# Eight score units of a second cross attention moved ahead of a linear layer, its first maxima placed between FFN tiles, and its third pack loaded under other waits

## The reference, cut to what matters

```python
x = x + L0_xattn(layernorm(x), ctx)          # self attention, cross attention, FFN (relu), norms g1, g2, g3
x = x + L0_ffn(layernorm(x))                 # a linear layer with a low rank part: "lin"
x = x + L1_xattn(layernorm(x), ctx, ctx, pad_mask, subsq_mask)   # the second cross attention
x = x + L1_ffn(layernorm(x))                 # experts: gated q, k, v products, attention, gated MLP
# L1_xattn: 16 heads of 16, scores / 4, masked places -1e9, softmax over T = 77 keys, times v
```

## Time and profile before

| | |
|---|---|
| runs before | median 1295.17 us (1292.96 to 1298.21, 3 runs) |
| profiled execution | 1296.56 us, span 1294.8 us, granted PE clock 0.942 |
| busy in the span | PE 1130.4 us (87%), DVE 834.1 (64%), ACT 556.0 (43%), POOL 261.0 (20%) |
| chain that ended last | PE on L726 12% of the span, DVE 0% |

### The profile page before, as it was taken

The page is one execution under the profiler, slowest core; times in us unless marked ns, Lnnn a source line. Parts: engine busy times, 40 slices in busy tenths (PEclk is TensorE's granted clock), DMA queues, the critical chain, the costliest instruction groups (busy, mean ns, idle before and its releaser), DMA issues. The chain is left out here.

```text
span 1294.8 us, 19733 instructions
## 1 busy us (share of the span) xinstructions
PE 1130.4 (87%) x6996; PEld 768.3 (59%) x6996; DVE 834.1 (64%) x1820; ACT 556.0 (43%) x1199; POOL 261.0 (20%) x429
## 2 busy tenths in 40 slices
PE   8789899988978788989868588899989788899999
PEld 4444333333333336667644256799978677789988
DVE  5486777877754667856654586676544566865555
ACT  6215666655646545445425343320023333543342
POOL 5012222222221045533212500000010113300000
PEclk8889999999989869999988789999989999999999
DMA  6750373330544502005615400001030000000000
GB/s 211 176 135 2 58 65 51 51 51 2 99 53 73 114 10 70 1 1 88 70 14 164 77 10 1 1 1 33 1 130 2 1 1 1 1 17 1 17 17 17
DMA packets 51217, 61.05 MB, mean 47 GB/s; under 512 B 16794, under 2 KB 40880, under 8 KB 50608
## 3 DMA queue, kind: packets, MB, share of 16 engines
q1 hardware_dynamic: 50688, 56.64, 22.6%
q0 software_dynamic: 432, 3.15, 0.7%
HBM read 44.02 MB, written 15.15 MB: 46 GB/s over the span
## 5 line engine op out<-in xcount | busy, mean ns | idle before, releaser
L726 PE MATMUL PS<-ARENA 128*17 128x512 f32 (+14 forms) x1720 | 299.4, 449 | 46.5 <-DVE ARENA L2062 15.5
L1585 ACT ACTIVATE ARENA<-PS 128x512 f32<-128x512 f32 (+3 forms) x384 | 169.9, 495 | 134.5 <-PE PS L726 132.3
L2062 DVE TENSOR_REDUCE ARENA<-PS 128x1 f32<-128x128 f32 (+7 forms) x256 | 182.7, 751 | 45.5 <-PE PS L726 43.7
L726 PEld LDWEIGHTS PS<-ARENA 128*17 128x17 f32 (+5 forms) x1720 | 87.6, 101 | 195.3 <-issue 107.1
L726 PE MATMUL PS<-WQKVP,TRR 128*128 128x384 f32 x512 | 137.8, 351 | 8.7 <-DVE ARENA L2323 7.4
L2515 POOL TENSOR_SCALAR_AFFINE_SELECT ARENA<-ARENA 128x128 f32<-128x128 f32 x256 | 74.0, 299 | 224.8 <-ACT ARENA L1585 222.9
L726 PEld LDWEIGHTS PS<-WQKVP,TRR 128*128 128x128 f32 x512 | 91.8, 191 | 17.9 <-DVE ARENA L2323 9.5
L726 PEld LDWEIGHTS PS<-W2P,INT 128*128 128x128 f32 x768 | 95.3, 188 | 2.9
L2483 POOL TENSOR_TENSOR rstd<-var,halves 128x4 f32<-128x4 f32 x36 | 38.4, 1068 | 285.5 <-DVE var L1851 193.7
L726 PE MATMUL PS<-W2P,INT 128*128 128x256 f32 x768 | 95.8, 280 | 0.0
L726 PE MATMUL PS<-TRR,W1P 128*128 128x512 f32 x256 | 87.2, 401 | 7.1 <-ACT BC L1502 7.1
(11 more groups left out here) (256 smaller groups left out, 1986.5 us busy)
## 6 DMA issues: line engine op xcount, KB each, us to landing
ARENA<-qk_parts SPq DMA_DIRECT2D x96, 128.0 KB, 5.6
ARENA<-xq_parts SPq DMA_DIRECT2D x48, 128.0 KB, 5.8
qk_parts<-ARENA SPq DMA_DIRECT2D x6, 768.0 KB, 3.3
ARENA<-yq_parts SPq DMA_DIRECT2D x36, 128.0 KB, 5.6
ARENA<-in_w SPq DMA_DIRECT2D x2, 2048.0 KB, 11.4
xq_parts<-ARENA SPq DMA_DIRECT2D x8, 384.0 KB, 2.6
yq_parts<-BC SPq DMA_DIRECT2D x8, 384.0 KB, 2.9
X<-in_x SPq DMA_DIRECT2D x4, 512.0 KB, 6.1
```

The lines of the kernel that those rows point to most:

```text
L726: return nc.tensor.matmul(o, lhsT, rhs, start=start, stop=stop, **kw)
L1585: ins = nc.scalar.activation(PROB[GRP * (step % 2) + j][:, 0:w], PS[:, uses[key][0], 0:w], ACT.Exp, scale=HD ** -0.5)
L2062: ins = v.tensor_reduce(negm[:, n % 2, TPB * j + st:TPB * j + st + 1], PS[:, bank:bank + 2, :].rearrange("p b s -> p (b s)")[:, 0:P * (st ...
```

## The change

The change does this:

- `expert_plan` takes a part. Part 0 is the first eight slots (units 0 to 7, `pv2` 0, `evac2` 0); PE and ACT run it in round 4 right after the queries of chunk 2, ahead of `t_lin` of chunk 3, whose 16 fill matmuls go. Part 1 is the rest.
- The eight maxima of chunk 0 and their turn go into round 3, between the last four `f2` tiles on PE; on DVE all eight stand ahead of the readout of `f2` tile 12, the turn ahead of that of tile 14.
- The eight maxima of chunk 1 and their turn take the old place of chunk 0's, behind `t_lin` of chunk 3 and ahead of `lin`.
- `context_values` and all four mask turns go into round 3, ahead of the last `f2` tiles; their banks now come from the ring. On DVE the context's values stand behind the norm `lin` of chunk 2.
- Chunk 2's and 3's maxima move to slots 18 to 21 and 25 to 28, 34 to 41; the late fourth chunk's work moves 8 slots back; the weight splits move to slots 25 to 39. Chunk 1's gate chain starts 8 ticks later.
- The third pack gets other pieces; SP loads it without waiting for the queries of chunk 3, with the rows of chunk 1 between its halves.

```diff
-WEIGHT_AT = (17, 19, 21, 23, 25, 28, 31, 34)
+WEIGHT_AT = (25, 27, 29, 31, 33, 35, 37, 39)
+FRONT, SECOND_CHAIN = 8, 8
+FRONT_MAXIMA = ((0, 1), (2, 3), (4, 5, 6, 7), ())
...
+    for m in range(4):
+        put(18 + m, "max2", 2, m, 0)
+        put(25 + m, "max2", 2, m, 1)
+        put(34 + m, "max2", 3, m, 0)
+        put(38 + m, "max2", 3, m, 1)
+    put(29, "neg2", 2)
+    put(42, "neg2", 3)
+    put(13, "late_norm", 3)
...
-            chains[t // 4] = p
+            chains[t // 4] = p + SECOND_CHAIN * (t // 4 == 1)
...
+        if (p < FRONT) != (part == 0):
+            continue
...
-        YLATE = ([H[:, 8 + 4 * k:12 + 4 * k, :].rearrange("p i f -> p (i f)") for k in range(2)]
-                 + [TR[:, k, N // 2:] for k in range(2)])
+        YLATE = [H[:, 8:12, :].rearrange("p i f -> p (i f)"), region(28624, 1024), region(30672, 1024),
+                 H[:, 12:16, :].rearrange("p i f -> p (i f)")]
```

TensorE (the values and masks ahead of the last `f2` tiles, then round 4):

```diff
                 for b in range(B):
-                    claim(("yv2", b), [6 + b])
+                    bank = wide(1)
+                    claim(("yv2", b), [bank])
...
                     for g in range(2):
-                        queries(s - 2, g, 4 + g, WQ3, "wq3")
+                        queries(s - 2, g, (2 if s == 4 else 4) + g, WQ3, "wq3")
                 if s == 4:
-                    second_maximum(0, 0, 0)
-                    second_maximum(0, 1, 0)
+                    cross_and_experts(0)
                 if 0 < s < 5:
-                    turn("t_lin", "lin", H, s - 1, wait=(0, 24, 6, 6, 16)[s])
+                    turn("t_lin", "lin", H, s - 1, wait=(0, 24, 6, 6, 0)[s])
                 if s == 4:
-                    for m in range(2, 8):
-                        second_maximum(0, m % 4, m // 4)
-                    second_turn(0)
+                    for m in range(8):
+                        second_maximum(1, m % 4, m // 4)
+                    second_turn(1)
...
+                if s == 3:
+                    context_values()
+                    for q in range(TILES // 4):
+                        turn_mask(q)
                 if s < 4:
                     pe.wait_ge(ht_ready, FCH * (s + 1))
                     pe.wait_ge(wf2_split, 4)
                     for i in range(4 * s, 4 * s + 4):
+                        if i >= TILES - 4:
+                            for m in FRONT_MAXIMA[i - TILES + 4]:
+                                second_maximum(0, m % 4, m // 4)
+                        if i == TILES - 1:
+                            second_turn(0)
                         claim(("f2", i), [6 + i % 2])
```

SyncE, ScalarE and VectorE:

```diff
                     sp.wait_ge(xparts_out[2 * c + g], 2 * 16)
+                    if c == 2 and g == 1:
+                        load_second_rows(sp, 1)
...
+                        if (c, g, h0) == (2, 1, GRP):
+                            drained(sp, ("t_xat", TILES - 1))
...
             send_second(2)
-            load_second_rows(sp, 1)
-            arrived(sp, ("q", "wq3", XCHUNKS - 1, 1))
             load_second(2)
...
+                if s == 4:
+                    cross_and_experts(0)
                 if 0 < s < 5:
                     normalize("lin", s - 1)
                     evacuate("t_lin", s - 1)
...
                 if s == 4:
                     for m in range(8):
-                        second_maximum(0, m % 4, m // 4)
-                    second_turn(0)
+                        second_maximum(1, m % 4, m // 4)
+                    second_turn(1)
+                    query_low(2, 0)
+                    query_low(2, 1)
...
+                if s == 3:
+                    context_values()
+                    for m in range(8):
+                        second_maximum(0, m % 4, m // 4)
                 if s < 4:
                     for i in batches[s]:
+                        if i == TILES - 2:
+                            second_turn(0)
                         arrived(dve, ("f2", i))
```

More of the change, by code:

```diff
@@ L296, in put @@
         slots.setdefault(at, []).append(op)
[L298 to L302, removed]
-    for half in range(2):
[L304 to L310, removed]
+    for m in range(4):
[6 more added lines that the diff above has]
+    put(13, "late_norm", 3)
+    for half in range(2):
+        put(15 + half, "late_turn", 3, half)
+        put(18 + half, "late_q", 3, half)
+        put(19 + half, "late_rest", 3, half)
+        put(21 + half, "late_mid", 3, half)
+        put(22 + half, "late_low", 3, half)
+    put(20, "load_weights", 0)
     for e, at in zip(WEIGHT_ORDER, WEIGHT_AT):
@@ L333, in expert_ticks, with expert_plan @@
     yield from products[done:]
-def expert_plan():
+def expert_plan(part):
     def add(t):
@@ L373, in expert_plan @@
                 yield (name, c, *half)
-    assert turned == TILES - 1
-    yield "turn_qk", TILES - 1
+    if part == 1:
+        assert turned == TILES - 1
+        yield "turn_qk", TILES - 1
 def build(nc, a, out):
@@ L496, in build @@
         YO = region(12288, 1024, "p (i f) -> p i f", i=4)
-        YOUT = [region(13312 + 512 * s, 512) for s in range(2)]
+        YOUT = [BC[:, 6 + 2 * s:8 + 2 * s, :].rearrange("p n f -> p (n f)") for s in range(2)]
         YV = W6[0:T, 616:616 + B * HEADS * VW].rearrange("p (b h e) -> p b h e", b=B, h=HEADS)
@@ L1065, in context_values @@
                 for b in range(B):
-                    claim(("yv2", b), [6 + b])
+                    bank = wide(1)
+                    claim(("yv2", b), [bank])
                     for k in range(KC):
-                        ins = mm(PS[0:T, 6 + b, 0:D], ctxT[:, k, T * b:T * b + T], W3[:, 1, k, :], start=k == 0, stop=k == KC - 1)
+                        ins = mm(PS[0:T, bank, 0:D], ctxT[:, k, T * b:T * b + T], W3[:, 1, k, :], start=k == 0, stop=k == KC - 1)
                     filled(ins, ("yv2", b))
@@ L1078, in turn_mask, with cross_and_experts @@
                 filled(ins, ("hide", q))
-            def cross_and_experts():
-                ring, products = 0, 0
+            def cross_and_experts(part):
+                ring, products = FRONT * part, 0
                 def narrow():
                     return wide(1) if products == 0 else wide(1) % 2
-                for op, n, *at in expert_plan():
+                for op, n, *at in expert_plan(part):
                     if op == "late_turn":
@@ L1099, in cross_and_experts @@
                         queries(n, at[0], wide(1), WQ3, "wq3")
-                    elif op == "hide":
-                        turn_mask(n)
                     elif op == "score2":
@@ L1107, in cross_and_experts @@
                             pe.wait_ge(ykeys_ones, 1)
-                            drained(pe, ("hide", 1))
-                        if (n, j) == (8, 0):
                             drained(pe, ("hide", 3))
@@ L1205, in _ @@
                         context(g, 4 + g, W3[:, 0, :, :], "wk3")
-            cross_and_experts()
+            cross_and_experts(1)
             loaded(pe, "wo")
@@ L1666, in turn_mask @@
             def turn_mask(q):
[L1668 to L1671, removed]
                 key = ("hide", q)
@@ L1688, in cross_and_experts @@
                         key = ("yv", n)
+                        if n == 0:
+                            normalized(act, "g3", TILES - 1)
+                        elif n == 1:
+                            drained(act, ("lin", TILES - 1))
                         arrived(act, key)
@@ L1751, in _ @@
                     query_middle(s - 2, 1)
-                if s == 4:
-                    turn_mask(0)
-                    turn_mask(1)
+                if s == 3:
+                    for q in range(TILES // 4):
+                        turn_mask(q)
                 if 0 < s < 4:
@@ L2270, in cross_and_experts @@
             def cross_and_experts():
-                for op, n, *at in expert_plan():
+                for op, n, *at in expert_plan(1):
                     if op == "max2":
@@ L2351, in _ @@
                     layernorm(X, H, batches[s - 1])
-                if s > 1:
+                if 1 < s < 4:
                     query_low(s - 2, 0)
                     query_low(s - 2, 1)
+                if s == 3:
+                    context_values()
+                    for m in range(8):
+                        second_maximum(0, m % 4, m // 4)
                 if s < 4:
                     for i in batches[s]:
+                        if i == TILES - 2:
+                            second_turn(0)
                         arrived(dve, ("f2", i))
```

8 lines of the change are left out of this document (1 added, 7 removed).

## The result

The changed kernel takes 1315.55 us (1306.72 to 1322.55, 4 runs) beside 1294.07 us (1292.52 to 1298.21, 4 runs) for the kernel before on the same chip: ratio 1.0157 [1.0091, 1.0224]. That is slower by about 21 us, where the forecast was +4.9 and its range ended at 1309. The profiled execution took 1306.72 us, span 1304.9 us, granted PE clock 0.936; PE is busy 1133.0 us of it. A few executions of the kernel before fell in a second, slower state of the chip and are left out of every median and ratio here.

The account below looks back on a forecast made before the run. PE is mostly busy from 770 us; before that, engine handovers with three holes bound the kernel. Terms 4.2 + 3.1 - 1.3 = +6.0, counted as +4.9 for uncertain half clock: 1300.0 us; forecast bounds 1294 to 1306, range 1286 to 1309.

Parts of the forecast that it names:

- terms 1 to 3: Front up to unit 8: last FFN add +17.1 us, unit 0 at 672.7 held by POOL's ones, unit 8 +4.2 us.
- term 3: First unit to unit 8: 24.7 us where 32 us stood, so unit 8 starts at 697.4, +4.2 us.
- term 1: Last four FFN tiles: DVE's add ends at 660.5 instead of 643.4, +17.1 us, 2.3 of it for half clock.
- term 4: Unit 8 to the turn of chunk 2's maxima: 34.4 us where 31.3 stood, +3.1 us, so +7.3 at the turn.
- at nothing: Items priced at zero: POOL's later weight splits, masks on ACT ahead of chunk 2's `xat`, chunk 1's later gate chain.
- the slow rival: SP's queue ahead of unit 16: rows of chunk 1 land 4 us later, clock halves; +13, 1308 us; chance 0.20.
- Term 5: Two DMA waits behind chunk 2's turn: first no shorter, fourth pack's wait of 3.16 us filled by 1.3; -1.3 us.
- the four cases: Forecast +1 to +9 (0.50), products stop waiting for DVE (0.20), late rows (0.20), hole truly filled (0.10).
- The fast one: First expert products stop waiting for DVE's weighted sums, 7.4 us, as chunk 1's chain starts later; about 1287 us; chance 0.20.
- The filled hole: Ahead of unit 0: the hole is truly filled and 7 us return; -1, 1294 us; chance 0.10.

Follow-up runs that it names:

- a1: Changed kernel, but POOL issues the two big expert weight loads only when the rows of chunk 1 have landed: 1307.22 us, ratio 1.0075 to before.
- a2: Changed kernel, but SP issues the rows of chunk 1 ahead of the sends of chunk 2: 1314.62 us, ratio 1.0133 to before.
- a6: Changed kernel with chunk 1's gate chain starting where it did before: 1320.04 us, ratio 1.0181 to before.
- a3: Changed kernel, but POOL writes the ones into the keys two norms earlier, behind `xat` of chunk 2: 1309.87 us, ratio 1.0101 to before.
- a4: Changed kernel without the eight units in front; they stand behind `lin` of chunk 3 again: 1306.12 us, ratio 1.0106 to before.
- c3: Changed kernel with weight loads behind chunk 1's rows, ones earlier, chunk 2's maxima four slots sooner and the front reordered: 1288.53 us, ratio 0.9917 to before.
- b1: Kernel before, with POOL's big weight loads delayed so they go out with the rows of chunk 1: 1300.96 us, ratio 1.0049 to before.
- a7: Changed kernel with 24 fill matmuls between the queries of chunk 2 and unit 0: 1314.47 us, ratio 1.0136 to before.

## Why the prediction was wrong

**Right: terms 1 to 3.** +15.6 at the last add (predicted +17.1), with the hole of 3.96 us (nearly 5) and the half clock behind it, and 1.23 us of wait ahead of tile 14 (2.4); unit 0 at 671.3 (672.7), held by POOL's ones with 7.5 us idle (7); unit 8 late by 5.4 us (4.2). The last is luck in part: term 3 took 27.3 us for 24.7, with unit 8 kept near its place by the early unit 0; 1.2 us of that are in the units and transposes, the rest in the turn and in `lin` (5.2 us where 4.4 was taken). The `f2` row at 4.26 us for 2.99 bears out the half clock in term 1: it ran so behind a wait for DVE's copy out of PSUM. It is no clear case against the Trainium skill (TensorE: Matmul & The Clock Gate, "Loop structure matters more than you think"), and neither was the earlier trace rows: its sentence on DVE's copy is about a loop whose next matmuls follow immediately. Here PE stood still first, for 3.96 and 6.99 us.

**Wrong: term 4, in the price of the rows of chunk 1.** It took "land 1.3" from a landing of rows that were alone (chunk 2's in before, from 734.21 to 735.52), and an idle time of 2.5 us. Send 2 was on time (683.80 + 10.68 = 694.5, predicted 694.9) and so was PE (it reached unit 16 at 703.61 - 8.41 = 695.20, which is 705.9; the forecast start was 706.9). SP had issued the last row at 695.63, which is 706.3, 1.8 us sooner than forecast. Only the landing was off, 7.98 us behind the last issue for 1.3, and I had not asked what else goes out then. The late `lin` of chunk 3 was followed to the units and to ACT's late norm; that POOL issues 2.5 MB behind the last tile of `lin` stood in the program and in the trace of before (678.99), and the list "at nothing" did not have it. `a1` takes the loads away and gives the check on the whole term: from unit 8 (690.25) to the turn (724.87) it takes 34.6 us, where the term says 34.4, and its parts fit too: PE busy 28.06 us (28.7) and idle 6.56 (5.7), at clock 1.00. With the loads in it, 48.5 (687.96 to 736.47).

**The second half of the miss is the clock.** I charged a half clock in the front and in the slow rival (3 us), none in the forecast behind unit 16. Behind the 8.41 us wait it cost 28.84 - 20.85 = 8.0 us of busy time, and it was down again behind the 1.64 us wait ahead of the second late queries.

**Term 5** said the first DMA wait is "no shorter" and the change touches none of it: the turn to unit 32 is 11.9 us for 11.0, small, and the wait for the fourth pack is 1.58 us for 3.16, 1.6 less where 1.3 was forecast. Behind unit 32 2.8 us came back in all; the waits for L2333 (5.1 for 7.4) are in it.

**The rivals.** The slow one had place and sign right (rows of chunk 1, unit 16, a clock that halves) and 1308 for its time; its cause was SP's queue, and `a2` shows that the queue alone gains little. It also priced the clock at 3 us, for 8.0 measured. The real partner of the collision, on POOL's queue, was in none of the four cases. The fast one fell: moving the chain is worth about 1 us (`a6`), not 7. The filled hole was not there in the change; `a3` shows what it is worth when made, 11 us.

**What stays open:** 8.8 us of the loss in `a4`, why the clock behind the first expert product differs between profiles of the same work, and how much of `c3`'s gain is due to the units in front.

## What to carry to other kernels

When a step is moved, list every instruction that hangs on its tick on every queue, the DMAs first, and then ask what is in flight at the new time: here one `drained` in POOL's list carried 2.5 MB onto six 8 KB transfers that had been alone. Work placed into a hole fills it only if its own operands are written before the hole begins; a `memset` two norms too late cost 11 us. And a moved block should be judged with its edges moved too: the same change was 1.6 to 1.8% slower as written and 0.8% faster with four edges mended.

## What the runs showed of the hardware

- Six transfers of 8 KB that land in 1.8 us alone take 6.6 us beside 2.5 MB of loads from another queue, in the changed kernel and in `b1` alike; a send of 384 KB takes 10.4 us beside the same loads and 2.5 alone. The loads themselves landed in 7.2 and 10.2 us beside the rows, 8.9 and 11.2 beside the send, and 9.6 and 12.9 beside half a pack (`a1`). The Trainium skill (DMA: Bandwidth & Descriptors, "Anatomy of one DMA — SWDGE (gpsimd) path") gives about 2 us as the fixed part of a transfer issued by GpSimd. The 1.8 us of these rows, which SyncE issues, are near it; the 6.6 us show how far that is from the price under load.
- After the 8.41 us wait the granted clock stood at 0.50 (1.2 GHz) from 702 to 712 us, as the Trainium skill (TensorE: Matmul & The Clock Gate, "Loop structure matters more than you think") says of a long wait for DMA. A hole of 2.31 us behind 5.34 us of fill left the units at half clock too (`a7`). The same 165 matmuls took 20.85 us and 28.84 us.
- Later in the changed kernel the granted clock was 1.00 from 714 to 717 us, over most of a 1.64 us wait, and 0.50 again from 718 to 720; the queries behind that wait took 3.55 us for 1.88.
- In unchanged code the granted clock differed between two executions for tens of microseconds, worth some 10 us; comparing spans without an anchor would have halved the loss.
